# A recurrence kernel whose fp32 state is streamed to TensorE as bf16 upper halves of its own words

## The chip, the cores and the metric

The kernel runs on one NeuronCore of a Trainium2 chip. The metric is the device time of one launch in microseconds. Five engines work side by side and meet only through semaphores: TensorE (PE, with its weight loads shown apart as PEld), VectorE (DVE), ScalarE (ACT), GpSimd (POOL) and SyncE (SP), which here starts the transfers.

## The reference, cut to what matters

```
x = x + moe(x, cond)          # 5 branches (4 experts, 1 shared), each gelu(x @ w1 + b1) @ w2 + b2
# then a gated recurrence over the 1024 time steps of x, batch 2, width 256:
def step(h, xs):              # xzt, xrt, xht are the projections of x, vz, vr, vh those of cond
    z  = sigmoid(xzt + h @ U_z + vz)
    r  = sigmoid(xrt + h @ U_r + vr)
    hh = tanh(xht + r * h @ U + vh)
    h_new = (1.0 - z) * h + z * hh
    return (h_new, h_new)
x = x + all h_new
```

Every step needs the state of the step before, so the 1024 steps are a chain. Within a step there are two products that stand one behind the other: `h @ U_r` must be there before `r * h @ U` can start. The product with `U_z` and the work of the experts are beside that chain.

## The kernel before

Features lie on the 128 partitions (width 256 is KC = 2 chunks `k`), batch and time on the free axis. The state of one step is therefore a 128x4 tile (2 chunks, 2 batch entries). The 1024 steps are cut into 64 bodies of 16 steps (`t` 0 to 15), and 4 bodies make a chunk of 64 steps. The experts' work for the next chunk is cut into fp32 matmuls of 128x128 on 128 columns ("units"), which a table deals out over the steps of the present chunk: each step has window 0, ahead of the candidate's product, and window 1, behind it; window 0 takes one unit and window 1 takes two (one, in every eighth step). Of the 1024 steps about 900 have a unit in window 0. Where there is no unit, bf16 matmuls on a constant tile fill the window (L887).

The recurrent weights are held as two fp16 tiles, `u_high` and `u_mid` (value minus `u_high`). The moving operand is held as two fp16 parts as well, HI and LO. A gate is then 8 "high" matmuls (2 output chunks, 2 input chunks, two weight tiles, all on the HI part) and 4 "low" ones (`u_high` on the LO part), all added up in PSUM (L873). The matmuls stream more columns than they need: the columns beyond the first two are zeros and add nothing (`H_FILL` = 20 for h, `FILL` = 56 for r*h).

One step goes as follows. DVE makes the new state three times with the same scan: into `h_parts` as fp16 (HI, L701), into PSUM as fp32 (`h_fresh`, L703), and into the history `h_hist` (L705). It subtracts HI from the PSUM copy to make LO (L708), and halves the state (L710). PE runs the 8 high matmuls of gate r, then 3 of gate z (`early`), waits for LO, and runs the 4 low ones of r. ACT makes the tanh of r (L481). DVE makes r*h twice, as fp16 (L684) and in PSUM as fp32 (`product`, L685), and subtracts for LO (L687). PE runs z's other matmuls, window 0, and then the candidate's 8 high and 4 low matmuls. ACT makes the candidate's tanh, DVE's next scan takes it. Between the two lie DVE's two operations on gate z (L690, L691).

The projected inputs of a body are put into PSUM ahead of the recurrent products by an identity matmul, once per gate and body ("inject", L859). For that GpSimd splits each body's fp32 inputs into three bf16 parts (L372 to L379). GpSimd also adds the finished body to its input (`h_true`, `out_feat`, L387, L392), PE turns it (`turn_body` in step `t` = 1), ACT copies it and SP stores it. GpSimd's third task is to scale the experts' activations (`scale_tile`, L298, 128x128 fp32, two inputs in SBUF).

The order on every engine is the order in which the code is written; nothing is rescheduled. DVE's operations wait on semaphores (`act_done`, `state`), PE's first matmul of each high and each low group on `part_ready`.

Of the kernel before, what the change touches and what calls it, by code (L numbers as in the profile page):

```python
# [44 lines left out]
FILL = 56  # L45
H_FILL = 20
# [3 lines left out]
def moe_gru_kernel(nc, x, cond, gate_w, gate_b, time_w, time_b, ew1, eb1, ew2, eb2, sw1, sb1, sw2, sb2,  # L50
# [45 lines left out]
    UNITS, GELUS, RESIDUALS, PIECES, FIRST_SPLIT = {}, {}, {}, {}, {}  # L96
    for c in range(CH - 1):
        slots = [(c * TC + s, window) for s in range(TC)
                 for window in ((0, 1) if s % 8 == 7 else (0, 1, 1))]
        for kind, f, i in side_work(c):  # L100
# [13 lines left out]
            if kind == PROJECT:  # L114
                after = at[0] + at[1]
                for m in range(KC):
                    PIECES[after + m] = [(f, i, m, b) for b in range(B)]
                FIRST_SPLIT[after + KC] = f
    FIRST_SPLIT = {max(step for step, g in FIRST_SPLIT.items() if g == f): f for f in range(1, CH)}
# [6 lines left out]
    with ctx:  # L126
# [30 lines left out]
        xrest = sb("xrest", [P, GATES * KC, SC])  # L157
        xsplit = sb("xsplit", [P, 3, GATES * KC, SC], BF16)
        h_hist = sb("h_hist", [P, ROUND, 2 * ST])
        h_true = sb("h_true", [P, KC, SC])  # L160
# [32 lines left out]
        HI, LO = range(2)  # L193
        blend = sb("blend", [P, 2 * ST])
        half_h = sb("half_h", [P, ST])
        body_mark = sb("body_mark", [P, 1])
# [10 lines left out]
        product = gate_ps[R][:, AT + ST:AT + 2 * ST]  # L207
        h_fresh = gate_ps[C][:, AT + 2 * ST:AT + 4 * ST]
        h_now = h_hist[:, :, :].rearrange("p s (e two) -> p s e two", two=2)[:, :, :, 1]
        h_fresh_v = h_fresh.rearrange("p (e two) -> p e two", two=2)[:, :, 1]  # L210
# [21 lines left out]
        pool_passed = sem("pool_passed")  # L232
# [29 lines left out]
        split_ready = sem("split_ready")  # L262
# [7 lines left out]
        body_h = sem("body_h")  # L270
        body_added = sem("body_added")
        h_unscaled = sem("h_unscaled")
# [4 lines left out]
        PARTS_STEP, STATE_STEP = 4, 6  # L277
# [24 lines left out]
        def _(sp):  # L302
# [6 lines left out]
            sp.sem_inc(out_written, 2 * 16)  # L309

# [12 lines left out]
            def store_body(n):  # L323

                sp.wait_ge(turned_copied, n + 2)
# [14 lines left out]
            sp.wait_ge(out_written, (CH * BODIES + 1) * 2 * 16)  # L340
# [3 lines left out]
        def _(pool):  # L344
# [10 lines left out]
            pool.sem_inc(split_ready, 1)  # L355
            pool.memset(out_feat[:, :, :], 0.0).then_inc(body_added, 1)
            CHAIN0, PER_SPLIT = 1, 3

            def wait_apart(semaphore, value):

                pool.wait_ge(semaphore, value)
                pool.sem_inc(pool_passed, 1)

            def split(c, j):

                n = c * BODIES + j
                chain = n * PER_SPLIT + CHAIN0
                src = xpart[:, c % 2, :, j * SC:(j + 1) * SC]
                if j == 0:
                    pool.wait_ge(xp_ready, (c + 1) * (GATES * KC * B) + 1)  # L370
                wait_apart(injected, n + 1)
                pool.tensor_copy(xsplit[:, 0, :, :], src).then_inc(pool_chain, 1)  # L372
                wait_apart(pool_chain, chain + 1)
                pool.tensor_tensor(xrest[:, :, :], src, xsplit[:, 0, :, :],
                                   ALU.subtract).then_inc(pool_chain, 1)
                wait_apart(pool_chain, chain + 2)
                pool.tensor_copy(xsplit[:, 1, :, :], xrest[:, :, :]).then_inc(pool_chain, 1)
                pool.wait_ge(pool_chain, chain + 3)
                pool.tensor_tensor(xsplit[:, 2, :, :], xrest[:, :, :], xsplit[:, 1, :, :],  # L379
                                   ALU.subtract).then_inc(split_ready, 1)  # L380

            def add_body(n):

                first = n % 2 * STEPS
                wait_apart(body_h, n + 1)
                for k in range(KC):
                    pool.tensor_scalar(h_true[:, k, :].rearrange("p (s b) -> p s b", b=B),  # L387
                                       h_now[:, first:first + STEPS, k * B:(k + 1) * B],
                                       h_unscale[:, :], None, ALU.mult).then_inc(h_unscaled, 1)
                wait_apart(h_unscaled, KC * (n + 3))  # L390
                wait_apart(turned, n + 1)
                pool.tensor_tensor(out_feat[:, :, :], h_true[:, :, :],  # L392
                                   feat[:, :, n * SC:(n + 1) * SC], ALU.add
                                   ).then_inc(body_added, 1)

# [18 lines left out]
            pool.wait_ge(scales_made, 1)  # L414
            pool.wait_ge(gate_scales_made, 2)
            split(0, 0)

            for step in range(T):
                n, t = divmod(step, STEPS)
                c, j = divmod(n, BODIES)  # L420
                if t == 0 and n > 0:
                    add_body(n - 1)
                if t == 3 and j < BODIES - 1:
                    split(c, j + 1)
                if step in FIRST_SPLIT:
                    split(FIRST_SPLIT[step], 0)
# [3 lines left out]
            add_body(CH * BODIES - 1)  # L430


        @block.scalar
        def _(act):
# [50 lines left out]
            def input_part(c, g, m, b):  # L485

                if m == 0 and b == 0:
                    act.wait_ge(xp_done, c * GATES + (g + 1))
                    if g == 0:
                        act.wait_ge(split_ready, max(c - 1, 0) * BODIES + 1)  # L490
# [30 lines left out]
            for step in range(T):  # L521
# [4 lines left out]
                if step % STEPS == 5:  # L526
                    copy_rows(step // STEPS)
                for piece in PIECES.get(step, ()):
                    input_part(*piece)
            copy_rows(CH * BODIES)  # L530
# [3 lines left out]
        def _(dve):  # L534
# [10 lines left out]
            dve.memset(p_parts[:, :, :, :], 0.0)  # L545
            dve.memset(h_parts[:, :, :, :], 0.0).then_inc(part_ready, PARTS_STEP)
            dve.memset(h_hist[:, :, :], 0.0)
            dve.sem_inc(h_unscaled, 2 * KC)
# [122 lines left out]

            def gru_body(n):
                first = n * STEPS
                for t in range(STEPS):
                    gate0 = (first + t) * GATES
                    s0 = (first + t + 1) * STATE_STEP
                    sq = lambda ap: ap.rearrange("p (m b) -> p m b", b=B)
                    tr, tz = sq(tanh_r), tanh_z
                    prev = sq(h_now[:, (first + t - 1) % ROUND, :])
                    p = lambda i: p_parts[:, i, :, 0:B]  # L680
# [9 lines left out]
                    dve.tensor_scalar(blend_v[:, :, 0], tz, 1.0, half_s[:, :], ALU.add, ALU.mult).then_inc(state, 1)  # L690
                    dve.scalar_tensor_tensor(blend_v[:, :, 1], tz, 1.0, half_h[:, :], ALU.subtract, ALU.mult  # L691
                                             ).then_inc(state, 1)
# [5 lines left out]
                    dve.wait_ge(state, s0 + 3)  # L698
                    if t == 0:
# [275 lines left out]
```

## Time and profile before

| | us |
|---|---|
| median of three runs | 2120.41 (2115.2 to 2125.93) |
| the profiled execution, as timed | 2111.95 |
| its span, first to last instruction | 2110.1 |
| first scan of the recurrence to the last | 85.94 to 2104.12 |

Busy shares of the span: PE 98%, PEld 86%, DVE 57%, ACT 35%, POOL 19%. Matmuls are pipelined, and a matmul of some 20 columns stands in the trace for about 0.18 us although the next one starts 0.025 us behind it; so PE's 98% doesn't say that PE has no time left. Starts are what is read below. An fp32 matmul stands in the trace as two records, each with its own weight load.

### The profile page before, as it was taken

Reading aid. Unit: us, or ns where it says so; the run is one execution under the profiler, and the core shown is the slowest. Engines: PE = TensorE matmul, PEld = TensorE weight load, DVE = VectorE, ACT = ScalarE, POOL = GpSimd, SP = SyncE. Lnnn points to the kernel's source line nnn. Section 1 sums busy time; section 2 is a strip of 40 time slices with the busy share of each in tenths; the row PEclk is TensorE's granted clock in tenths of the full one; section 3 lists DMA queues with packets and bytes.
Section 4 is the critical chain, followed back from the end, with each engine's and each line's share of the span. In section 5 each row is a group of like instructions: output and inputs, shape, how many; then the busy total and the mean of one; then the engine's idle time right before and its main releaser. Section 6 shows DMA issues by size and latency. Waiting matters only on the chain.

```text
span 2110.1 us, 105994 instructions
## 1 busy us (share of the span) xinstructions
PE 2069.1 (98%) x43624; PEld 1817.8 (86%) x43624; DVE 1201.6 (57%) x10446; ACT 732.4 (35%) x3977; POOL 395.9 (19%) x931
## 2 busy tenths in 40 slices
PE   7999999999999999999999999999999999999998
PEld 6998988989888898988888888898988889888665
DVE  6455555555555555555555555555555555555555
ACT  2433333333333333333333333333333333333222
POOL 3121212121121211212122121211212122120010
PEclk8999999999999999999999999999999999999999
DMA  8000000000000000000000000000000000000000
GB/s 285 2 4 5 5 4 5 4 4 5 5 4 5 5 4 5 5 4 5 5 4 4 5 4 4 4 4 4 5 5 4 5 4 4 5 5 4 4 4 4
DMA packets 16931, 23.90 MB, mean 11 GB/s; under 512 B 3584, under 2 KB 15159, under 8 KB 16444
## 3 DMA queue, kind: packets, MB, share of 16 engines
q1 hardware_dynamic: 15280, 17.05, 2.5%
q8 instruction: 341, 5.59, 1.1%
q14 instruction: 146, 1.20, 0.2%
q10 hardware_dynamic: 1164, 0.07, 0.0%
HBM read 15.01 MB, written 2.10 MB: 8 GB/s over the span
## 4 chain that ended last, share of the span: by engine, by line
PE 94%; issue 2%; DVE 2%; ACT 1%; POOL 0%; POOLq 0%; DVEq 0%; ACTq 0%
PE c_ps L873 21%; PE r_ps L873 19%; PE y_ps L822 17%; PE up_ps L806 17%; PE z_ps L873 14%; PE xp_ps L833 2%; PE up_ps L887 2%; PE xp_ps L887 1%; DVE p_parts L684 1%; ACT r_ps L481 1%; PE rows_ps L854 1%; DVE h_parts L701 1%; DVE hidden L298 0%; ACT c_ps L481 0%; PE y_ps L795 0%
## 5 line engine op out<-in xcount | busy, mean ns | idle before, releaser
L873 PE MATMUL z_ps<-h_parts,u_high 128*128 128x20 f16 x8192 | 566.6, 178 | 0.0
L873 PE MATMUL r_ps<-h_parts,u_high 128*128 128x20 f16 (+1 forms) x8192 | 545.8, 172 | 10.4 <-DVE h_parts L701 0.2
L873 PEld LDWEIGHTS r_ps<-h_parts,u_high 128*128 128x128 f16 x8192 | 419.6, 96 | 154.9 <-DVE h_parts L701 86.3
L873 PE MATMUL c_ps<-p_parts,u_high 128*128 128x56 f16 (+1 forms) x8192 | 532.0, 178 | 11.0
L822 PE MATMUL y_ps<-hidden,down_w 128*128 128x128 f32 x2560 | 524.9, 301 | 4.5 <-DVE hidden L298 4.5
L806 PE MATMUL up_ps<-feat,up_w 128*128 128x128 f32 x2560 | 527.1, 302 | 0.0
L873 PEld LDWEIGHTS c_ps<-p_parts,u_high 128*128 128x128 f16 x8192 | 418.3, 96 | 106.5 <-DVE p_parts L684 33.6
L684 DVE SCALAR_TENSOR_TENSOR p_parts<-r_ps,h_hist 128x4 f16<-128x4 f32 x1024 | 168.4, 164 | 483.8 <-ACT r_ps L481 483.8
L873 PE MATMUL z_ps<-h_parts,u_mid 128*128 128x20 f16 x4096 | 438.3, 178 | 0.0
L873 PEld LDWEIGHTS z_ps<-h_parts,u_high 128*128 128x128 f16 x8192 | 423.5, 95 | 0.0
L481 ACT ACTIVATE r_ps<-r_ps 128x4 f32<-128x4 f32 x1024 | 161.8, 158 | 640.0 <-PE r_ps L873 636.1
L701 DVE TENSOR_TENSOR_SCAN h_parts<-c_ps,blend 128x8 f16<-128x8 f32 x1024 | 178.2, 174 | 344.7 <-ACT c_ps L481 340.4
L822 PEld LDWEIGHTS y_ps<-hidden,down_w 128*128 128x128 f32 x2560 | 367.2, 190 | 5.9 <-issue 3.4
L806 PEld LDWEIGHTS up_ps<-feat,up_w 128*128 128x128 f32 x2560 | 369.5, 191 | 0.4 <-issue 0.2
L481 ACT ACTIVATE c_ps<-c_ps 128x4 f32<-128x4 f32 x1024 | 161.8, 158 | 584.4 <-PE c_ps L873 584.4
L873 PE MATMUL c_ps<-p_parts,u_mid 128*128 128x56 f16 x4096 | 350.2, 187 | 0.0
L873 PE MATMUL r_ps<-h_parts,u_mid 128*128 128x20 f16 x4096 | 336.6, 178 | 0.0
L873 PEld LDWEIGHTS z_ps<-h_parts,u_mid 128*128 128x128 f16 x4096 | 295.6, 96 | 0.0
L873 PEld LDWEIGHTS c_ps<-p_parts,u_mid 128*128 128x128 f16 x4096 | 260.7, 96 | 0.7
L873 PEld LDWEIGHTS r_ps<-h_parts,u_mid 128*128 128x128 f16 x4096 | 256.5, 97 | 0.0
L476 ACT ACTIVATE hidden<-up_ps,small_cols 128x128 f32<-128x128 f32 x640 | 234.5, 366 | 41.0 <-PE up_ps L806 39.9
L690 DVE TENSOR_SCALAR blend<-z_ps,half_s 128x4 f32<-128x4 f32 x1024 | 218.9, 214 | 0.0
(137 smaller groups left out, 2274.8 us busy)
## 6 DMA issues: line engine op xcount, KB each, us to landing
up_w<-in_L_cond_ew SPq DMA_DIRECT2D x4, 1024.0 KB, 12.0
down_w<-in_L_cond_ew SPq DMA_DIRECT2D x4, 1024.0 KB, 13.2
x_rows<-in_x SPq DMA_DIRECT2D x8, 256.0 KB, 5.1
out<-out_rows SPq DMA_DIRECT2D x128, 16.0 KB, 1.8
up_w<-in_L_cond_sw SPq DMA_DIRECT2D x1, 1024.0 KB, 15.7
down_w<-in_L_cond_sw SPq DMA_DIRECT2D x1, 1024.0 KB, 11.8
cf<-in_L_cond_C_r SPq DMA_DIRECT2D x1, 256.0 KB, 5.9
cf<-in_L_cond_C_z SPq DMA_DIRECT2D x1, 256.0 KB, 6.1
```

Of the source, the lines that this page charges most:

```text
L476: act.activation(hidden[:, i % LAG, :], up_ps[i % 2][:, 0:COLS], ACT.Gelu_apprx_tanh, bias=small_cols[:, ROW_B1 + e * HT + j:ROW_B1 + e * ...
L481: act.activation((c_now, tanh_r, tanh_z)[(g + 1) % GATES].rearrange("p (m b) -> p m b", b=B), gate_v[g][:, :, step % STEPS, :], ACT.Tanh, ...
L684: dve.scalar_tensor_tensor(p(HI), tr, 1.0, prev, ALU.add, ALU.mult).then_inc(part_ready, 1)
L690: dve.tensor_scalar(blend_v[:, :, 0], tz, 1.0, half_s[:, :], ALU.add, ALU.mult).then_inc(state, 1)
L701: dve.tensor_tensor_scan(h_parts[:, HI, 0, :], cand, blend[:, :], 0.0, ALU.mult, ALU.add).then_inc(part_ready, 1)
L806: last = mm(up_ps[i % 2][:, 0:COLS], up_w[:, e, k, j * P:(j + 1) * P], feat[:, k, f * COLS:(f + 1) * COLS], start=(k == 0), stop=(k == KC ...
L822: last = mm(y_ps[:, m * COLS:(m + 1) * COLS], down_w[:, e, j, m * P:(m + 1) * P], hidden[:, i % LAG, :], start=False, stop=(m == KC - 1), ...
L833: last = mm(xp_ps[:, m * COLS:(m + 1) * COLS], wx[:, g, k, m * P:(m + 1) * P], feat[:, k, f * COLS:(f + 1) * COLS], start=(m == 0 and k == 0),
L854: last = pe.transpose(rows_ps[0:SC, k * P:(k + 1) * P], out_feat[:, k, :], ident[:, :])
L873: return mm(gate_ps[g][:, m * SC + t * B:m * SC + t * B + width], w[:, g, k, m * P:(m + 1) * P], moving, start=False, stop=i == LO and k = ...
L887: mm(idle_ps[:, 0:IDLE_FILL[window]], ident16[:, :], keep_warm[:, 0:IDLE_FILL[window]], start=True, stop=True, skip_group_check=True)
```

## The change

TensorE now streams the state and r*h out of the fp32 words themselves. DVE writes the state as fp32 into `h_words` (one word in each group of eight, the rest zeros), and PE reads the same bytes as bf16 from the upper half of that word on: 14 bf16 values, the first being the value's upper half and the others zeros, for each of two batch entries. The low part is the fp32 word minus its own bf16 view, as fp16.

```
-        p_parts = sb("p_parts", [P, 2, KC, FILL], F16)
-        h_parts = sb("h_parts", [P, 2, FILL // B, 2 * ST], F16)
+        p_words = sb("p_words", [P, ST + 1, WORDS])
+        h_words = sb("h_words", [P, ST + 1, 2 * WORDS])
+        p_low = sb("p_low", [P, ST + 1, 2 * WORDS], F16)
+        h_low = sb("h_low", [P, ST + 1, 2 * WORDS], F16)
...
+        high = lambda words: words[:, :, :].bitcast(BF16)
+        p_moving, h_moving = high(p_words)[:, :, 1:1 + RUN], high(h_words)[:, :, 2 * WORDS + 1:2 * WORDS + 1 + RUN]
...
-                    dve.scalar_tensor_tensor(p(HI), tr, 1.0, prev, ALU.add, ALU.mult).then_inc(part_ready, 1)
-                    dve.scalar_tensor_tensor(sq(product), tr, 1.0, prev, ALU.add, ALU.mult).then_inc(state, 1)
-                    dve.wait_ge(state, s0 + 1)
-                    dve.tensor_tensor(p(LO), sq(product), p(HI), ALU.subtract).then_inc(part_ready, 1)
+                    dve.scalar_tensor_tensor(p_full, tanh_r, 1.0, h_now[:, (first + t - 1) % ROUND, :],
+                                             ALU.add, ALU.mult).then_inc(part_ready, 1)
+                    dve.wait_ge(part_ready, parts0 + 1)
+                    dve.tensor_tensor(p_rest, p_full, p_high, ALU.subtract).then_inc(part_ready, 1)
...
+                    if n > 0 and 2 <= t < 2 + KC:
+                        output(n - 1, t - 2)
...
-                    dve.tensor_tensor_scan(h_parts[:, HI, 0, :], cand, blend[:, :], 0.0, ALU.mult, ALU.add
+                    dve.tensor_tensor_scan(h_pairs, cand, blend[:, :], 0.0, ALU.mult, ALU.add
                                            ).then_inc(part_ready, 1)
-                    dve.tensor_tensor_scan(h_fresh, cand, blend[:, :], 0.0, ALU.mult, ALU.add
-                                           ).then_inc(state, 1)
                     dve.tensor_tensor_scan(h_hist[:, (first + t) % ROUND, :], cand, blend[:, :], 0.0, ALU.mult, ALU.add
                                            ).then_inc(state, 1)
-                    dve.tensor_tensor(h_parts[:, LO, 0, :], h_fresh, h_parts[:, HI, 0, :],
-                                      ALU.subtract).then_inc(part_ready, 1)
-                    dve.tensor_scalar(half_h[:, :], h_fresh_v, -0.5, None, ALU.mult).then_inc(state, 1)
+                    dve.wait_ge(part_ready, parts0 + 3)
+                    dve.tensor_tensor(h_rest, h_full, h_high, ALU.subtract).then_inc(part_ready, 1)
+                    dve.tensor_scalar(half_h[:, :], h_full, -0.5, None, ALU.mult).then_inc(state, 1)
```

PE's matmuls on h, on r*h and z's low ones now have 28 columns, 2 runs of 14. The two batch entries stay interleaved in PSUM, so one run writes every second fp32 word. The weights stay fp16; the high part beside them is bf16. The injection is one fp32 identity matmul on the projected input itself, and GpSimd's splits are gone. The addition of the finished body is two DVE operations (`output`, at `t` = 2 and 3 of the next body), and `turn_body` stands at `t` = 5.

```
+                last = mm(gate_ps[g][:, 0:KC * SC], ident[:, :],
+                          xpart[:, c % 2, g * KC:(g + 1) * KC, j * SC:(j + 1) * SC],
+                          start=True, stop=True, skip_group_check=True)
...
+                    cols = gate_ps[g][:, at:at + B * run].rearrange("p (f b) -> p b f", b=B)
+                    last = mm(cols, w[:, g, k, m * P:(m + 1) * P], part[:, k * B:(k + 1) * B, 0:run], start=False,
+                              stop=products is LOW_PRODUCTS and k == KC - 1, skip_group_check=True)
...
-                    early = 0 if t == 0 else 3
-                    for product in HIGH_PRODUCTS[:early]:
-                        recur(Z, t, h_parts, HI, product, H_FILL)
                     pe.wait_ge(part_ready, before_n + 4)
-                    for product in LOW_PRODUCTS:
-                        last_mm = recur(R, t, h_parts, LO, product, B)
-                    last_mm.then_inc(preact, 1)
-                    for product in HIGH_PRODUCTS[early:]:
-                        recur(Z, t, h_parts, HI, product, H_FILL)
+                    recur(R, t, h_low, LOW_PRODUCTS, 1).then_inc(preact, 1)
+                    recur(Z, t, h_moving, HIGH_PRODUCTS, RUN)
```

What stands where, at the places that matter (a scan stands in these rows as SCALAR_TENSOR_TENSOR). DVE, one whole step, before:

```order
416 L684 SCALAR_TENSOR_TENSOR p_parts<-r_ps,h_hist 128x2x2 [waits state,act_done]
417 L685 SCALAR_TENSOR_TENSOR r_ps<-r_ps,h_hist 128x4
418 L687 TENSOR_TENSOR p_parts<-r_ps,p_parts 128x2x2 [waits state]
419 L690 TENSOR_SCALAR blend<-z_ps,half_s 128x4 [waits act_done]
420 L691 SCALAR_TENSOR_TENSOR blend<-z_ps,half_h 128x4
421 L701 SCALAR_TENSOR_TENSOR h_parts<-c_ps,blend 128x8 [waits state,act_done]
422 L703 SCALAR_TENSOR_TENSOR c_ps<-c_ps,blend 128x8
423 L705 SCALAR_TENSOR_TENSOR h_hist<-c_ps,blend 128x8
424 L708 TENSOR_TENSOR h_parts<-c_ps,h_parts 128x8 [waits state]
425 L710 TENSOR_SCALAR half_h<-c_ps 128x4
```

and of the changed kernel:

```order
408 L632 SCALAR_TENSOR_TENSOR p_words<-r_ps,h_hist 128x4 [waits state,act_done]
409 L635 TENSOR_TENSOR p_low<-p_words 128x4 [waits part_ready]
410 L638 TENSOR_SCALAR blend<-z_ps,half_s 128x4 [waits act_done]
411 L640 SCALAR_TENSOR_TENSOR blend<-z_ps,half_h 128x4 [waits state]
412 L650 SCALAR_TENSOR_TENSOR h_words<-c_ps,blend 128x8 [waits state,act_done]
413 L652 SCALAR_TENSOR_TENSOR h_hist<-c_ps,blend 128x8
414 L655 TENSOR_TENSOR h_low<-h_words 128x4 [waits part_ready]
415 L656 TENSOR_SCALAR half_h<-h_words 128x4
```

Ten operations became eight: the second copy of r*h and the second copy of the state are gone from between the first write and the subtraction.

PE in an ordinary step, from the high matmuls of gate r to its low ones, before:

```order
3024 L873 MATMUL r_ps<-h_parts,u_high 128x20
3025 L873 MATMUL r_ps<-h_parts,u_mid 128x20
3026 L873 MATMUL z_ps<-h_parts,u_high 128x20
3027 L873 MATMUL z_ps<-h_parts,u_mid 128x20
3028 L873 MATMUL z_ps<-h_parts,u_high 128x20
3029 L873 MATMUL r_ps<-h_parts,u_high 128x2 [waits part_ready]
3030 L873 MATMUL r_ps<-h_parts,u_high 128x2 x3
```

and of the changed kernel:

```order
1821 L822 MATMUL r_ps<-h_words,u_high 128x2x14
1822 L822 MATMUL r_ps<-h_words,u_mid 128x2x14
1823 L822 MATMUL r_ps<-h_low,u_high 128x2 [waits part_ready]
1824 L822 MATMUL r_ps<-h_low,u_high 128x2 x3
1825 L822 MATMUL z_ps<-h_words,u_high 128x2x14
1826 L822 MATMUL z_ps<-h_words,u_mid 128x2x14
```

The three matmuls of gate z that stood ahead of the wait now stand behind r's low ones, in front of window 0.

PE in the first step of a body, around the injection for gate z, before:

```order
2827 L873 MATMUL r_ps<-h_parts,u_high 128x20
2828 L873 MATMUL r_ps<-h_parts,u_mid 128x20
2829 L859 MATMUL z_ps<-xsplit,ident16 128x64 x3
2830 L873 MATMUL r_ps<-h_parts,u_high 128x2 [waits part_ready]
2831 L873 MATMUL r_ps<-h_parts,u_high 128x2 x3
```

and of the changed kernel:

```order
1787 L822 MATMUL r_ps<-h_words,u_high 128x2x14
1788 L822 MATMUL r_ps<-h_words,u_mid 128x2x14
1789 L808 MATMUL z_ps<-xpart,ident 128x64
1790 L822 MATMUL r_ps<-h_low,u_high 128x2 [waits part_ready]
1791 L822 MATMUL r_ps<-h_low,u_high 128x2 x3
```

Three bf16 matmuls ahead of r's low ones became one fp32 matmul in the same place.

## Rows read from the trace of the kernel before

**Rows 1.** Timeline, DVE: first and last scan (start us, us, what).

```profile
85.94 0.17 DVE L701 TENSOR_TENSOR_SCAN h_parts<-c_ps,blend 128x8 f16<-128x8 f32 x1 [0.37 <-ACT c_ps L481]
...
2104.12 0.17 DVE L701 TENSOR_TENSOR_SCAN h_parts<-c_ps,blend 128x8 f16<-128x8 f32 x1 [0.34 <-ACT c_ps L481]
```

**Rows 2.** Timeline, DVE, one step, from its scan to the next.

```profile
1013.32 0.17 DVE L701 TENSOR_TENSOR_SCAN h_parts<-c_ps,blend 128x8 f16<-128x8 f32 x1 [0.34 <-ACT c_ps L481]
1013.41 0.17 DVE L703 TENSOR_TENSOR_SCAN c_ps<-c_ps,blend 128x8 f32<-128x8 f32 x1
1013.49 0.15 DVE L705 TENSOR_TENSOR_SCAN h_hist<-c_ps,blend 128x8 f32<-128x8 f32 x1
1013.61 0.17 DVE L708 TENSOR_TENSOR h_parts<-c_ps,h_parts 128x8 f16<-128x8 f32 x1
1013.70 0.15 DVE L710 TENSOR_SCALAR half_h<-c_ps 128x4 f32<-128x4 f32 x1
1014.32 0.17 DVE L684 SCALAR_TENSOR_TENSOR p_parts<-r_ps,h_hist 128x4 f16<-128x4 f32 x1 [0.47 <-ACT r_ps L481]
1014.39 0.16 DVE L685 SCALAR_TENSOR_TENSOR r_ps<-r_ps,h_hist 128x4 f32<-128x4 f32 x1
1014.59 0.16 DVE L687 TENSOR_TENSOR p_parts<-r_ps,p_parts 128x4 f16<-128x4 f32 x1
...
1015.29 0.17 DVE L701 TENSOR_TENSOR_SCAN h_parts<-c_ps,blend 128x8 f16<-128x8 f32 x1 [0.34 <-ACT c_ps L481]
```

**Rows 3.** Timeline, PE, the same step: matmuls of r, z, window 0, candidate.

```profile
1013.55 0.18 PE L873 MATMUL r_ps<-h_parts,u_high 128*128 128x20 f16 x1
...
1013.74 0.18 PE L873 MATMUL r_ps<-h_parts,u_mid 128*128 128x20 f16 x1
...
1013.84 0.24 PE L873 MATMUL r_ps<-h_parts,u_high 128*128 128x2 f16 x4
...
1014.17 0.47 PE L806 MATMUL up_ps<-feat,up_w 128*128 128x128 f32 x2
1014.54 0.20 PE L873 MATMUL c_ps<-p_parts,u_high 128*128 128x56 f16 x1
...
1014.73 0.19 PE L873 MATMUL c_ps<-p_parts,u_mid 128*128 128x56 f16 x1
1014.81 0.25 PE L873 MATMUL c_ps<-p_parts,u_high 128*128 128x2 f16 x4
```

**Rows 4.** Timeline, PE, the first step of a body.

```profile
999.90 0.18 PE L873 MATMUL r_ps<-h_parts,u_mid 128*128 128x20 f16 x1
999.93 0.25 PE L859 MATMUL z_ps<-xsplit,ident 128*128 128x64 bf16 x3
1000.01 0.24 PE L873 MATMUL r_ps<-h_parts,u_high 128*128 128x2 f16 x4
...
1000.50 0.47 PE L806 MATMUL up_ps<-feat,up_w 128*128 128x128 f32 x2
1000.81 0.19 PE L873 MATMUL c_ps<-p_parts,u_high 128*128 128x56 f16 x1
```

**Rows 5.** Fill matmuls: one pair in the timeline; their group by line and shape.

```profile
2103.76 0.59 PE L887 MATMUL up_ps<-keep_warm,ident 128*128 128x512 bf16 x2
...
L887 PE MATMUL up_ps<-keep_warm,ident 128*128 128x512 bf16 x170 | 50.3, 377 | 0.0
```

**Rows 6.** Timeline: DVE and GpSimd operations that overlap, ahead of the recurrence.

```profile
81.12 0.29 DVE L298 TENSOR_TENSOR hidden<-hidden,gate_scale 128x128 f32<-128x128 f32 x1 [0.52 <-ACT hidden L476]
82.02 0.46 DVE L298 TENSOR_TENSOR hidden<-hidden,gate_scale 128x128 f32<-128x128 f32 x1 [0.60 <-ACT hidden L476]
...
81.78 0.55 POOL L379 TENSOR_TENSOR xsplit<-xrest,xsplit 128x192 bf16<-128x192 f32 x1
```

**Rows 7.** GpSimd scaling: one of the step in rows 2, and a group.

```profile
1013.65 0.40 POOL L298 TENSOR_TENSOR hidden<-hidden,expert_w 128x128 f32<-128x128 f32 x1 [1.57 <-ACT hidden L476]
...
L298 POOL TENSOR_TENSOR hidden<-hidden,gate_scale 128x128 f32<-128x128 f32 x235 | 108.3, 461 | 477.5 <-ACT hidden L476 477.5
```

More of the change, by code:

```diff
@@ L354, in _ @@
                                       bass.bass_isa.ReduceOp.max).then_inc(umax_shared, 1)
[L355 to L394, printed above, removed]
             pool.wait_ge(expert_w_made, 1)
@@ L488, in input_part @@
                     act.wait_ge(xp_done, c * GATES + (g + 1))
[L489 to L490 removed]
+                    if g == 0 and c >= 2:
+                        act.wait_ge(injected, (c - 1) * BODIES)
                 act.activation(
@@ L525, in _ @@
                     gelu(f, i)
-                if step % STEPS == 5:
-                    copy_rows(step // STEPS)
+                if step % STEPS == 8 and step > STEPS:
+                    copy_rows(step // STEPS - 1)
                 for piece in PIECES.get(step, ()):
                     input_part(*piece)
-            copy_rows(CH * BODIES)
+            copy_rows(CH * BODIES - 1)
         @block.vector
@@ L724, in _ @@
                 gru_body(n)
+            dve.wait_ge(state, (T + 1) * STATE_STEP)
+            for k in range(KC):
+                output(CH * BODIES - 1, k)
         @block.tensor
@@ L855, in turn_body, with inject @@
                 last.then_inc(turned, 1)
-            def inject(g, last_of_body):
-                for i in range(3):
-                    last = mm(gate_ps[g][:, 0:KC * SC], ident16[:, :],
-                              xsplit[:, i, g * KC:(g + 1) * KC, :].rearrange("p k n -> p (k n)"),
-                              start=(i == 0), stop=(i == 2), skip_group_check=True)
-                if last_of_body:
+            def inject(g, n):
+                c, j = divmod(n, BODIES)
+                if g == R and j == 0:
+                    pe.wait_ge(xp_ready, (c + 1) * (GATES * KC * B) + 1)
+                last = mm(gate_ps[g][:, 0:KC * SC], ident[:, :],
+                          xpart[:, c % 2, g * KC:(g + 1) * KC, j * SC:(j + 1) * SC],
+                          start=True, stop=True, skip_group_check=True)
+                if g == C:
                     last.then_inc(injected, 1)
@@ L866, in _, with recur @@
             LOW_PRODUCTS = [(m, k, u_high) for m in range(KC) for k in range(KC)]
-            def recur(g, t, part, i, product, width):
-                m, k, w = product
-                moving = (p_parts[:, i, k, 0:width] if part is p_parts else
-                          h_parts[:, i, 0:width // B, (2 * k) * B + 1:(2 * k + 2) * B:2])
-                return mm(gate_ps[g][:, m * SC + t * B:m * SC + t * B + width],
-                          w[:, g, k, m * P:(m + 1) * P], moving, start=False,
-                          stop=i == LO and k == KC - 1, skip_group_check=True)
+            def recur(g, t, part, products, run):
+                for m, k, w in products:
+                    at = m * SC + t * B
+                    cols = gate_ps[g][:, at:at + B * run].rearrange("p (f b) -> p b f", b=B)
+                    last = mm(cols, w[:, g, k, m * P:(m + 1) * P], part[:, k * B:(k + 1) * B, 0:run], start=False,
+                              stop=products is LOW_PRODUCTS and k == KC - 1, skip_group_check=True)
+                return last
             def gap_work(n, t, window):
-                if t == 1 and window == 1:
-                    turn_body(n)
+                if t == 5 and window == 1 and n > 0:
+                    turn_body(n - 1)
                 units = UNITS.get((n * STEPS + t, window), ())
```

102 lines of the change are left out of this document (36 added, 66 removed).

## The prediction, made before the changed kernel ran

> **What bounds the kernel now.** I read the timeline first, since 98% for PE is made of overlapping records. The first scan of the recurrence starts at 85.94 and the last at 2104.12 [rows 1]: 1023 steps of 1.973 us, which is 96% of the span, so the question is one step. DVE's rows of one step [rows 2] beside PE's [rows 3], as distances from the scan's start: scan 0; PE's first r matmul 0.23, the eighth 0.42; the subtraction L708 0.29; r's low matmuls 0.52; r*h (L684) 1.00; its second copy (L685) 1.07; its subtraction (L687) 1.27; the candidate's high matmuls 1.22 to 1.41, its low ones 1.49; next scan 1.97. Each link starts a fixed distance behind the one before. From the subtraction L708 to r's low matmuls it is 0.23, from these to L684 0.48 (four matmuls, ACT's tanh, DVE), from L687 to the candidate's low matmuls 0.22, from these to the next scan 0.48. The step is a chain of latencies through DVE, PE and ACT. PE is close behind it, though: its eight r matmuls end at 0.42, and I note that three z matmuls fill the time to 0.52.
>
> **DVE's second copies, the gain.** Before, L708 starts 0.29 behind the scan, because it waits for the second scan (0.09 later, 0.17 long, then 0.03) [rows 2]. Afterwards it needs the first scan alone: 0.17 + 0.03 = 0.20 to 0.21. Its bounds are 0.19 (if a scan into SBUF takes the 0.15 of L705) and 0.23 (if the spread-out fp32 writes cost 0.02). Likewise L687 started 0.27 behind L684 and will start 0.16 + 0.035 = 0.20 behind it. That is 0.08 and 0.07 off the chain. L708's and L687's own durations I keep at 0.17 and 0.16.
>
> **PE takes over at three places.** R's low matmuls are ready at 0.205 + 0.23 = 0.435; PE has issued the eight high ones at 0.42 + 0.025 = 0.445. So 0.445, against 0.52 before: 0.075 gained. With nothing waited for, the four follow at 0.025 each, 0.005 less than behind a wait. So r*h starts at 0.445 + 0.475 = 0.92. The candidate's high matmuls are ready 0.22 later, at 1.14. PE by then has to issue 4 low r, 12 z (three of them moved behind the wait by the change) and window 0. Those are 16 x 0.025 = 0.40, so the fp32 unit starts at 0.845. In rows 4 a unit keeps PE from 1000.50 to 1000.81, 0.31, and the next matmul really waits for it there. So they start at 1.155, PE 0.015 late. This holds in the 900 steps with a unit in window 0. The eight took 0.19 with a longer first gap behind a wait [rows 3]; with none, 7 x 0.026 = 0.18. Hence the low ones at 1.155 + 0.18 + 0.025 = 1.36 (they are ready at 0.92 + 0.20 + 0.22 = 1.34), and the next scan at 1.36 + 0.47 = 1.83. A step is 1.83 instead of 1.97: 0.14 x 1023 = **143 us gained**. Window 1 keeps its 0.6 us between the candidate's low matmuls and the next scan plus 0.23, so its two units stay hidden.
>
> **The injection, a loss.** In a body's first step the three bf16 matmuls move r's low ones to 0.11 behind the last high one, against 0.025 [rows 4]; this was hidden but for about 0.03, since LO was late anyway. An fp32 matmul is two passes with two weight loads; a unit's 0.31 less 0.05 for 64 instead of 128 columns in its last pass is 0.26. It stands on the path: r's low matmuls come at 0.42 + 0.27 = 0.69 instead of 0.445, 0.245 later. The injection for the candidate stands ahead of window 0's unit and puts two more fp32 weight loads (0.31 less a last pass of about 0.10, so 0.21) and a gap of 0.02 in front of the candidate: 0.23. Together 0.47 x 64 = 30 us, less 0.03 x 64 = 2 before: **28 us lost**. The injection for r is in the last step's window 1, which has only one unit (0.31 + 0.26 in 0.6): nothing.
>
> **Edits at nothing.** GpSimd's splits and body additions were never waited for in the loop. DVE's `output` (two operations on 32 columns, below 0.29, the 128-column row of rows 6) fits in the 0.5 us between L691 and the scan. `turn_body` costs at `t` = 5 what it cost at `t` = 1. The tail loses one GpSimd stage of some 0.6 us. The added wait ahead of L640 is on DVE's own earlier operation and is met. The head is unchanged.
>
> **The unknown term: 28 columns in every second PSUM word.** No matmul of before writes PSUM with a step. Twenty columns (r) and fifty-six (candidate) both go by 0.025 to 0.027 [rows 3]; long ones cost (0.59 - 0.377) / 512 = 0.42 ns a column [rows 5]. If a stepped column is worth one, 28 stay at 0.025. If it is worth two, they are the 56 of before, 0.026. On the bounding path lie 8 r, 12 z and 8 candidate matmuls, so 1 ns each is 0.028 x 1024 = 29 us. I take the mean of the two readings, 0.3 ns, 9 us. Lower end 0, upper end open (below). The mixed types (fp16 weights, bf16 moving) are not in the trace either. The nearest rows are bf16 matmuls among fp16 ones at no visible cost [rows 4]; I take 0.
>
> **Sum.** 2112 - 143 + 28 - 1 + 9 = 2005 us in terms of the profiled execution. The median shown is 1.004 of that execution (2120.4 / 2112), so **2013 us**. Within this case: scans shorter by 0.02 give -20, matmuls slower by 0.5 ns more +15, strided DVE operations 0.03 longer at one place +30: 1978 to 2060.
>
> **Rival 1, slower: the stepped PSUM writes.** One mechanism: a stepped column is worth three or more. Then 28 of them are at least 84 columns, 28 x 0.42 = 12 ns above the 56-column matmul; 12 x 29 = 345, so about 2360. It decides from 4 ns: 108 us are to be eaten up at 29 us per ns, so at matmuls above 0.029 to 0.030 the kernel is slower. For it: no row excludes it. Against it: half the rate is the plainest price of writing one word of each two. I give 0.16 to this, and 0.08 to something between (2120 to 2200). The Trainium skill (Advanced Engine Details and Errata, PSUM Cachelines) says that PSUM lines hold two fp32 values and that any non-contiguous pattern slows matmuls significantly. No run here shows it yet; by its line size a line per value is the factor two, which by the numbers above is 2022, and "significantly" read as more is this rival.
>
> **Rival 2: DVE and GpSimd in each other's way.** A DVE operation on two SBUF tensors takes 0.29 alone and 0.46 beside a GpSimd operation that runs to 82.33, 0.15 before DVE's end [rows 6]. Before, all small DVE operations of a step had one tensor in PSUM; now L635 and L655 have both in SBUF, and L656 goes from SBUF to SBUF. GpSimd scales in some 450 steps (235 of one kind, about as many of the other), 0.40 to 0.46 each [rows 7], from 0.33 behind the scan. L655 would run from 0.21 to 0.37, so it is first; L635 at 1.12 comes after GpSimd's end at 0.79 or a little more. L656 (from 0.29) may lose the race and end at 0.95, which delays L684 by 0.03 to 0.1: 15 to 45 us, 2028 to 2058. Were L655 itself caught, it would be 0.37 x 450 = 165 us, 2180. Chance 0.10 for a visible cost, nearly all of it the smaller one. The Trainium skill (SBUF — State Buffer, Who interferes with whom) states this rule, a lock held for the whole instruction whenever DVE has two SBUF inputs and GpSimd reads SBUF; rows 6 agree with it.
>
> **Rival 3: the change doesn't do what it says.** The separate copies were started 0.08 apart, overlapped; if each new operation on spread-out words (scan, r*h, both subtractions) is 0.03 longer, 0.06 to 0.12 of the 0.14 is gone: 2070 to 2125. The three kinds of scan differ by only 0.02 [rows 2], which speaks against it. Chance 0.08.
>
> **How the numbers follow.** Forecast 0.58; rival 1 0.16, its milder form 0.08; rival 2 0.10; rival 3 0.08. The range from 1975 to 2190 takes all but the strong form of rival 1 and the tails, about 0.8. This kernel's runs can tell 0.5%, 10 us, from no change. Faster by more: 0.58 + 0.10 + 0.07 = 0.75 less 0.02 for the tails, 0.73; within: 0.04; slower: 0.16 + 0.07 = 0.23.
>
> **What would show it.** In the profile of the changed kernel: L655 0.20 to 0.21 behind the scan (a GpSimd row beside a longer L655 or L656 is rival 2); r's low matmuls directly behind its eighth; starts of 28-column matmuls 0.025 to 0.026 apart (0.030 or more is rival 1); L635 0.20 behind L632; the first step of a body about 0.47 longer than the others; 1.83 from scan to scan. What would make it wrong most easily is the spacing of the matmuls, since PE now bounds three places of the step.

## The result and the profile after

| | before | changed |
|---|---|---|
| median, us | 2122.23 (4 runs, 2115.2 to 2125.93) | 2024.10 (4 runs, 2022.93 to 2025.53) |
| profiled execution, span | 2110.1 | 2022.6 |
| first to last scan | 85.94 to 2104.12 | 84.71 to 2017.92 |
| mean from scan to scan | 1.973 | 1.890 |

The changed kernel takes 0.954 of the time, 95% interval 0.952 to 0.957: 4.6% faster. The forecast was 2013, the range 1975 to 2190. Of the 87.5 us of span, 85 come from the recurrence; the tail gives 1.3, and the head's 1.2 is less than it differs by among the kernels below that share it (first scan at 83.3 to 86.3).

The medians are 98 us apart, the two profiled executions 88 (2111.95 and 2024.38). Of 11 later runs of the kernel before, the time and the mean granted clock are on record: from 2110.1 us at 0.996 to 2129.7 at 0.979, longer with each lower clock but for one run at 0.999 (2111.4). The changed kernel's stood at 0.996 to 1.000. So some 10 us of the medians' distance go with the clock, and the change itself is worth about 4.1%; why the kernel before loses clock is open.

DVE of one step in the timeline of the changed kernel (start us, us, engine, line, operation, out<-in), to be held against [rows 2]:

```profile
1009.11 0.18 DVE L650 TENSOR_TENSOR_SCAN h_words<-c_ps,blend 128x8 f32<-128x8 f32 x1 [0.30 <-ACT c_ps L422]
1009.20 0.16 DVE L652 TENSOR_TENSOR_SCAN h_hist<-c_ps,blend 128x8 f32<-128x8 f32 x1
1009.32 0.18 DVE L655 TENSOR_TENSOR h_low<-h_words 128x4 f16<-128x4 f32 x1
...
1010.04 0.17 DVE L632 SCALAR_TENSOR_TENSOR p_words<-r_ps,h_hist 128x4 f32<-128x4 f32 x1 [0.47 <-ACT r_ps L422]
1010.24 0.18 DVE L635 TENSOR_TENSOR p_low<-p_words 128x4 f16<-128x4 f32 x1
...
1010.97 0.18 DVE L650 TENSOR_TENSOR_SCAN h_words<-c_ps,blend 128x8 f32<-128x8 f32 x1 [0.30 <-ACT c_ps L422]
```

The state's subtraction starts 0.21 behind the scan (0.29 before), that of r*h 0.20 behind the product (0.27 before), and the step takes 1.86 (1.97 before). PE of the same step, against [rows 3]:

```profile
1009.35 0.20 PE L822 MATMUL r_ps<-h_words,u_high 128*128 128x28 bf16 x1
...
1009.54 0.19 PE L822 MATMUL r_ps<-h_words,u_mid 128*128 128x28 bf16 x1
1009.56 0.25 PE L822 MATMUL r_ps<-h_low,u_high 128*128 128x2 f16 x4
1009.68 0.19 PE L822 MATMUL z_ps<-h_words,u_high 128*128 128x28 bf16 x1
...
1009.99 0.47 PE L767 MATMUL y_ps<-hidden,down_w 128*128 128x128 f32 x2
1010.29 0.19 PE L822 MATMUL c_ps<-p_words,u_high 128*128 128x28 bf16 x1
...
1010.50 0.24 PE L822 MATMUL c_ps<-p_low,u_high 128*128 128x2 f16 x4
```

R's low matmuls stand 0.02 behind its last high one, where they stood 0.10 behind it before: PE has no gap there any more. The candidate's high ones stand 0.30 behind the fp32 unit, the distance at which a waiting matmul follows a unit in [rows 4]; they are held by PE, not by DVE. The first step of a body, against [rows 4]:

```profile
1020.77 0.19 PE L822 MATMUL r_ps<-h_words,u_mid 128*128 128x28 bf16 x1
1020.80 0.41 PE L808 MATMUL z_ps<-xpart,ident 128*128 128x64 f32 x2
1021.05 0.25 PE L822 MATMUL r_ps<-h_low,u_high 128*128 128x2 f16 x4
...
1021.47 0.41 PE L808 MATMUL c_ps<-xpart,ident 128*128 128x64 f32 x2
1021.72 0.44 PE L751 MATMUL up_ps<-feat,up_w 128*128 128x128 f32 x2
1021.99 0.19 PE L822 MATMUL c_ps<-p_words,u_high 128*128 128x28 bf16 x1
```

The low matmuls of r come 0.28 behind the last high one (0.11 before). The scans around it are at 1020.34 and 1022.67, 2.33 apart.

### The profile page after: what moved, and what is told of

The parts are those of the page before. It is cut to its first block, busy times and chain, and to the rows that moved or that the text cites. A ratio compares the mean times of both kernels' runs of the same rounds, so it can differ in the third digit from the quotient of the medians.

```text
span 2022.6 us, 102778 instructions
## 1 busy us (share of the span) xinstructions
PE 1988.2 (98%) x43359; PEld 1816.3 (90%) x43430; DVE 1142.4 (56%) x8464; ACT 737.2 (36%) x3976; POOL 217.8 (11%) x482
## 4 chain that ended last, share of the span: by engine, by line
PE 96%; DVE 2%; issue 1%; ACT 1%; DMA 0%; SPq 0%; POOL 0%; DVEq 0%; ACTq 0%
PE r_ps L822 20%; PE y_ps L767 17%; PE up_ps L751 17%; PE z_ps L822 17%; PE c_ps L822 16%; PE xp_ps L778 2%; PE up_ps L836 2%; PE xp_ps L836 1%; PE c_ps L808 1%; PE z_ps L808 1%; PE rows_ps L800 1%; DVE h_words L650 1%; ACT c_ps L422 1%; PE r_ps L808 1%; DVE hidden L294 1%
## 5 line engine op out<-in xcount | busy, mean ns | idle before, releaser
L822 PE MATMUL r_ps<-h_words,u_high 128*128 128x28 bf16 x4096 | 362.8, 190 | 9.3 <-DVE h_words L650 0.3
L822 PE MATMUL c_ps<-p_words,u_high 128*128 128x28 bf16 x4096 | 354.0, 188 | 1.2
L822 PE MATMUL r_ps<-h_words,u_mid 128*128 128x28 bf16 x4096 | 350.2, 187 | 0.0
L822 PE MATMUL z_ps<-h_words,u_mid 128*128 128x28 bf16 x4096 | 350.2, 187 | 0.0
L822 PE MATMUL c_ps<-p_words,u_mid 128*128 128x28 bf16 x4096 | 350.2, 187 | 0.0
L822 PE MATMUL z_ps<-h_words,u_high 128*128 128x28 bf16 x4096 | 349.4, 187 | 0.0
L822 PEld LDWEIGHTS c_ps<-p_words,u_high 128*128 128x128 f16 x4096 | 264.0, 96 | 25.3 <-DVE p_words L632 24.1
L822 PE MATMUL z_ps<-h_low,u_high 128*128 128x28 f16 x4096 | 270.8, 187 | 0.0
L822 PEld LDWEIGHTS r_ps<-h_words,u_mid 128*128 128x128 f16 x4096 | 260.0, 96 | 0.0
L822 PEld LDWEIGHTS c_ps<-p_words,u_mid 128*128 128x128 f16 x4096 | 259.3, 96 | 0.7
```

The source lines that it names most:

```text
L822: last = mm(cols, w[:, g, k, m * P:(m + 1) * P], part[:, k * B:(k + 1) * B, 0:run], start=False, stop=products is LOW_PRODUCTS and k == KC ...
```

## The experiments

All are changes to the changed kernel; its time is called "2024". An interval is given where there are several times; of the others there is one, and the changed kernel's own four lie within 0.13%.

**The stepped PSUM writes.** Three kernels vary the columns or the step.

```
-RUN = 2 * WORDS - 2
+RUN = 10
```

> Each run of columns is 10 instead of 14, so a recurrent matmul streams 20 columns into every second PSUM word instead of 28. Theory (a stepped column costs as much as two): 20 count as 40, below what the 56 of before cost, so starts go from 0.026 to 0.025 us apart; the 28 matmuls between the scan and the candidate's low ones save 0.02 to 0.03 a step, 2024 becomes 1998 to 2008. Rival (the spacing of 0.026 comes from the mixed types or from the words' distance, not from the columns): no change, 2024.

Measured: 2012.85 us, 0.948 of the kernel before (interval 0.941 to 0.955). And with 44 columns:

```
-WORDS = 8
+WORDS = 12
```

> Each run of columns is 22 instead of 14 (words 12 apart instead of 8), so 44 stepped columns. Theory (a stepped column costs as much as two): 44 count as 88, about 0.42 ns each, starts 0.037 to 0.040 us apart, +0.3 to +0.4 us a step, 2330 to 2430 us. Rival (a stepped column costs one): 44 are still below 56, starts stay at 0.026, 2024 us.

Measured: 2368.2 us. The z group of the two kernels, and of the changed one between them, by line and shape (busy us, mean ns of one):

```profile
L822 PE MATMUL z_ps<-h_words,u_high 128*128 128x20 bf16 x4096 | 337.2, 179 | 0.0
```

```profile
L822 PE MATMUL z_ps<-h_words,u_high 128*128 128x28 bf16 x4096 | 349.4, 187 | 0.0
```

```profile
L822 PE MATMUL z_ps<-h_words,u_high 128*128 128x44 bf16 x4096 | 444.5, 210 | 0.0
```

A matmul of 28 stepped columns stands in the trace for 187 ns, which is what the 56 unstepped columns of the kernel before took (0.19 in [rows 3]), and 20 stepped ones for 179, as 20 unstepped ones did (0.18). The starts say the same. Within the z group they are in the mean 25.0 ns apart with 20 columns, 25.8 with 28 and 38 with 44. These rows are of the 44:

```profile
1009.54 0.21 PE L822 MATMUL z_ps<-h_words,u_high 128*128 128x44 bf16 x1
1009.58 0.21 PE L822 MATMUL z_ps<-h_words,u_mid 128*128 128x44 bf16 x1
1009.62 0.21 PE L822 MATMUL z_ps<-h_words,u_high 128*128 128x44 bf16 x1
```

At 0.42 ns a column [rows 5], 88 columns are 37 ns: a column into every second PSUM word costs about as much as two. That rests on one size above the floor of 25 ns; 44 columns without a step were not run, but the 56 of the kernel before stand 25.8 ns apart. The short run gained 11 us where 16 to 26 were expected. Its step went from 1.857 to 1.846 only. R's low matmuls were by then waiting for DVE's subtraction (its start 0.21, its length 0.177, and 0.06 until they start: 0.45), and the last of the four starts at 0.536 in both kernels, so the spacing of r's eight no longer counted. In the same way the candidate's four start 0.015 earlier, but the last of them only 0.008.

The third kernel takes the step out of PSUM and puts the jump on the reading side:

```
-                    cols = gate_ps[g][:, at:at + B * run].rearrange("p (f b) -> p b f", b=B)
-                    last = mm(cols, w[:, g, k, m * P:(m + 1) * P], part[:, k * B:(k + 1) * B, 0:run], start=False,
+                    cols = gate_ps[g][:, at:at + B * run].rearrange("p (f b) -> p f b", b=B)
+                    last = mm(cols, w[:, g, k, m * P:(m + 1) * P], part[:, k * B:(k + 1) * B, 0:run].rearrange("p b f -> p f b"), start=False,
```

> The two batch entries are interleaved on the moving side instead of in PSUM: PSUM is written without a step, and the moving operand is read with a jump of 32 or 64 bytes from column to column. Theory (the PSUM step is what makes 28 columns cost like 56, and jumps on the reading side are free): starts 0.025 apart, 1998 to 2008 us. Rival (jumps on the reading side cost more than the step in PSUM): starts over 0.030 apart, above 2060 us.

Measured: 2111.9 us. The theory fell: its z matmuls start 28.2 ns apart, more than the 25.8 with the step in PSUM, and the ordinary step is 1.915. The rival's 30 was not reached, though its time was. In ten stretches of 7 to 17 us the granted clock fell to its lower level of 1.2 GHz, which it does nowhere in the changed kernel's recurrence. The 972 steps outside them are longer than the changed kernel's by 53 us in all, 0.055 each; the 51 steps in them by 35, of which 32 go with the clock. Stretches of this kernel's profile (the column behind POOL is the granted clock):

```profile
182.00:300.00 118.00, 117.31 (x2559) 109.88 (x2557) 66.83 (x496) 42.76 (x236) 13.35 (x31) 1.00 0.02 4
301.00:318.00 17.00, 17.00 (x262) 16.31 (x262) 7.26 (x54) 4.83 (x27) 0.80 (x2) 0.51 0.01 2
318.00:430.00 112.00, 111.31 (x2421) 104.00 (x2422) 62.92 (x468) 40.13 (x220) 12.93 (x30) 1.00 0.02 4
```

In the 17 us at a mean of 0.51 PE got 15.4 matmuls a microsecond done, in the stretch before 21.7. Before the fall at 301 us PE was busy for 117.3 of 118 us, as in the changed kernel (497.0 of 500). All ten falls begin at the same place of a chunk of 64 steps, from 0.3 us ahead of to 1.1 us behind the scan that ends its third body, some 6 us behind two steps whose windows hold bf16 fill matmuls in place of fp32 units. The changed kernel has the same work there and keeps its clock; why it fell here and not there is open.

**DVE's second copies.** Both are put back, and the subtractions wait for them:

```
+                    dve.scalar_tensor_tensor(product, tanh_r, 1.0, h_now[:, (first + t - 1) % ROUND, :],
+                                             ALU.add, ALU.mult).then_inc(copied, 1)
+                    dve.wait_ge(copied, 2 * (first + t) + 1)
-                    dve.wait_ge(part_ready, parts0 + 1)
...
+                    dve.tensor_tensor_scan(h_fresh, cand, blend[:, :], 0.0, ALU.mult, ALU.add
+                                           ).then_inc(copied, 1)
...
-                    dve.wait_ge(part_ready, parts0 + 3)
+                    dve.wait_ge(copied, 2 * (first + t) + 2)
```

> The second copy of r*h and the second scan into PSUM are put back between the first write and the subtraction, which waits for them; nothing reads them otherwise. Theory (the gain is these two operations off the chain): subtraction of the state 0.29 behind the scan instead of 0.21, that of r*h 0.27 behind instead of 0.20, r's low matmuls at 0.53 instead of 0.45; a step of 1.99 instead of 1.857, about 2155 us. Rival (PE bounds the step by itself and would have given the gain without this): the second copies hide behind PE, at most 1.90 a step, below 2070 us.

Measured: 2160.1 us, 1.017 of the kernel before (interval 1.010 to 1.025). The ordinary step is 2.00. The rival is out: PE alone gives nothing, and the two copies are worth 136 us, more than the whole difference between the kernels. With the copies back the step is 0.033 longer than the 1.967 before, so the rest of the change costs that much. The rows place it: r's last low matmul starts at 0.616 instead of 0.602, and the candidate's low ones 0.236 instead of 0.220 behind the start of their subtraction, which takes 0.178 instead of 0.164. DVE in one step of this kernel, with GpSimd's operation beside it:

```profile
1012.04 0.18 DVE L655 TENSOR_TENSOR_SCAN h_words<-c_ps,blend 128x8 f32<-128x8 f32 x1 [0.35 <-ACT c_ps L425]
...
1012.32 0.18 DVE L662 TENSOR_TENSOR h_low<-h_words 128x4 f16<-128x4 f32 x1
1012.41 0.43 DVE L663 TENSOR_SCALAR half_h<-h_words 128x4 f32<-128x4 f32 x1
1013.04 0.17 DVE L635 SCALAR_TENSOR_TENSOR p_words<-r_ps,h_hist 128x4 f32<-128x4 f32 x1 [0.20 <-ACT r_ps L425]
...
1012.36 0.46 POOL L297 TENSOR_TENSOR hidden<-hidden,gate_scale 128x128 f32<-128x128 f32 x1 [1.88 <-ACT hidden L420]
```

The subtraction is 0.28 behind the scan, as wanted. The halving of the state, due at 0.37 and now behind GpSimd's start at 0.32, takes 0.43 instead of 0.16 and ends 0.02 behind GpSimd; 454 of the 1024 are like this. It costs nothing: their steps are 2.00 long, as the others. This answers the milder half of rival 2 of the prediction, in which the held halving was to delay the next product: here it ends at 0.80, and the product starts at 1.00.

**The fp32 injection.** First with one bf16 matmul per gate on inputs kept as bf16:

```
-        xpart = sb("xpart", [P, 2, GATES * KC, COLS])
+        xpart = sb("xpart", [P, 2, GATES * KC, COLS], BF16)
...
-                last = mm(gate_ps[g][:, 0:KC * SC], ident[:, :],
+                last = mm(gate_ps[g][:, 0:KC * SC], ident16[:, :],
```

> The projected inputs are kept as bf16 and injected by one bf16 matmul per gate and body, so the low 16 bits of the projected inputs are left out. Theory (the fp32 injection costs 0.47 us in each body's first step): the step from a body's last scan to the next body's first, 2.33 us in the changed kernel against 1.86 in the others, falls to 1.86 to 1.90; 27 to 30 us less, 1994 to 1997 us. Rival (the first step is long for another reason, such as the wait for the state or for the projected inputs): it stays above 2.2 us and the time above 2018.

Measured: 1997.2 us, and a body's last scan is 1.906 from the next body's first (2.327 in the changed kernel). The 27 us are the injection's. Then the fp32 matmul of gate z moved ahead:

```
-                    if t == 0:
-                        inject(Z, n)
...
                         inject(R, n + 1)
+                        pe.wait_ge(state, (n + 1) * STEPS * STATE_STEP + 2)
+                        inject(Z, n + 1)
...
+            inject(Z, 0)
```

> The fp32 injection for gate z is moved from between r's high and low matmuls to the end of the last step's window 1, behind the one for r. Theory (PE has no time left in these two steps, so its work only moves): 0.24 us less behind the scan, but window 1 then holds 0.33 + 0.27 + 0.24 in 0.63 and gives 0.2 back; 2018 to 2026 us. Rival (what costs is the place on the path alone): 64 x 0.24 = 15 us less, 2009 us.

Measured: 2016.65 us, just below the theory's 2018. The step is mostly 2.162 instead of 2.327. Of the 0.24 to 0.25 that the path alone would have gained, 0.165 are left, since r's first matmul, behind the fuller window 1, starts at 0.332 instead of 0.232. In 14 of the 63 such steps it is 2.28 or more; the mean is 2.184 instead of 2.314, which makes 8 us.

**GpSimd beside DVE.** Less of it, and more of it:

```
...
+            if engine is not dve_engine[0]:
+                part = hidden[:, i % LAG, 0:B]
+                engine.tensor_tensor(part, part, expert_w[:, e, :], ALU.mult).then_inc(scaled, 1)
+                return
...
```

> GpSimd scales only the first two columns of each tile instead of 128, so nearly all of its scaling is left out. Theory (GpSimd's work meets DVE's two SBUF-to-SBUF operations in a handful of steps only): 2020 to 2024 us. Rival (each GpSimd operation costs DVE some time): 450 steps x 0.03 or more, below 2010 us.

Measured: 2020.7 us: GpSimd's scaling costs the changed kernel 0 to 4 us in all. In the changed kernel three of DVE's rows of L635, L655 and L656 are held. One is this (DVE and GpSimd timeline):

```profile
120.61 0.18 DVE L650 TENSOR_TENSOR_SCAN h_words<-c_ps,blend 128x8 f32<-128x8 f32 x1 [0.29 <-ACT c_ps L422]
...
120.82 0.39 DVE L655 TENSOR_TENSOR h_low<-h_words 128x4 f16<-128x4 f32 x1
...
120.78 0.40 POOL L294 TENSOR_TENSOR hidden<-hidden,expert_w 128x128 f32<-128x128 f32 x1 [1.46 <-ACT hidden L417]
```

GpSimd started 0.17 behind the scan here, 0.04 ahead of the subtraction, which then lasted until GpSimd was done. In 459 of 467 cases GpSimd starts 0.32 behind the scan, when the subtraction runs already.

```
                         scale_tile(pool, f, i)
...
+                        pool.tensor_tensor(scrap[:, :], ones[:, :], ident[:, :], ALU.mult).then_inc(scrapped, 1)
```

> Behind each scaling GpSimd runs a second operation of the same size on three other SBUF tiles, so it is busy from 0.32 to about 1.15 to 1.25 us behind the scan instead of 0.32 to 0.78. Theory (a DVE operation with two SBUF inputs waits while GpSimd runs): the subtraction of r*h, due at 1.13, is held until GpSimd ends in the 450 steps with a scaling, rows of 0.2 to 0.3 us instead of 0.178; 5 to 40 us more, 2029 to 2064 us. Rival (they don't get in each other's way): 2024 us.

Measured: 2022.9 us, no difference. The second operation starts at 0.68 to 0.75 and ends at 1.13 or 1.14 in 227 steps and at 1.19 or 1.20 in 231. The subtraction of r*h, at 1.13, was held in 5 steps of 1024. So in some 230 steps GpSimd ran on for 0.06 into the subtraction, which took its 0.178 all the same. DVE and GpSimd of one such step:

```profile
1010.59 0.18 DVE L642 TENSOR_TENSOR p_low<-p_words 128x4 f16<-128x4 f32 x1
...
1010.14 0.46 POOL L378 TENSOR_TENSOR scrap<-ones,ident 128x128 f32<-128x128 f32 x1
```

The expectation had the end about right; what it had wrong is that so short an overlap would cost something. With two added operations, on a buffer of two halves:

```
                         scale_tile(pool, f, i)
+                        for _ in range(2):
+                            if scraps[0] > 1:
+                                pool.wait_ge(scrapped, scraps[0] - 1)
+                            pool.tensor_tensor(scrap[:, scraps[0] % 2, :], ones[:, :], ident[:, :], ALU.mult).then_inc(scrapped, 1)
+                            scraps[0] += 1
```

> As with the doubled GpSimd work, but with two added operations behind each scaling, so GpSimd runs from 0.32 to about 1.5 us behind the scan and the last of its three operations starts at about 1.03 to 1.1, ahead of the subtraction of r*h at 1.13. Theory (whoever starts first holds the other up to its end): that subtraction takes 0.4 to 0.6 us instead of 0.178 in about 450 steps, +0.25 to +0.4 us each, 2130 to 2200 us. Rival (the few long rows seen so far had another reason): below 2035 us.

Measured: 2085.7 us. The subtraction of r*h was held in 262 steps, not in 450: in the others the third operation started behind it. DVE of one such step in the timeline, with GpSimd's row of the two added operations:

```profile
1001.12 0.17 DVE L658 TENSOR_TENSOR_SCAN h_words<-c_ps,blend 128x8 f32<-128x8 f32 x1 [0.30 <-ACT c_ps L430]
...
1002.29 0.40 DVE L643 TENSOR_TENSOR p_low<-p_words 128x4 f16<-128x4 f32 x1
...
1001.79 0.87 POOL L378 TENSOR_TENSOR scrap<-ones,ident 128x128 f32<-128x128 f32 x2
```

And the group of all these subtractions, by line (busy us, mean ns of one, idle us before them):

```profile
L643 DVE TENSOR_TENSOR p_low<-p_words 128x4 f16<-128x4 f32 x1024 | 248.7, 243 | 34.8
```

262 x 0.26 is 68 us; 61 were measured. The held ones end 0.03 behind GpSimd's operation. So a GpSimd operation that starts first holds the subtraction up to its own end, except where its end is as near as the 0.06 above. The changed kernel is not hurt because of where GpSimd's operation happens to start.

**A version that beats both.** It has 20 columns (as in the first experiment), gate z's injection at the body's end (as above), and lighter windows around the body's border:

```
-RUN = 2 * WORDS - 2
+RUN = 10
...
-                 for window in ((0, 1) if s % 8 == 7 else (0, 1, 1))]
+                 for window in {0: (1, 1), 15: (0,)}.get(s % STEPS, (0, 1, 1))]
...
-                if not units:
+                if not units and (t, window) not in ((0, 0), (STEPS - 1, 1)):
```

> A version meant to beat both: 20 instead of 28 columns; the fp32 injection for gate z in the last step's window 1; no unit in that window and none in window 0 of a body's first step (they move to the windows that had one unit in every eighth step). Theory: 11 us for the columns as measured alone, 7 for the injection as measured alone, and the body's first step down from 2.16 (with the earlier injection) to about 1.86, 0.3 x 64 = 19 us; 1984 to 1990 us. Rival (the moved units cost elsewhere what they save there): 2000 us or more.

Measured: 1984.9 us, 0.940 of the kernel before (0.938 to 0.941). And the same without the change of `RUN`, so with the 28 columns kept:

> As the version meant to beat both, with the 28 columns kept. Theory: 11 us above it, 1994 to 2001 us, the step from a body's last scan to the next body's first at 1.86 to 1.92 us. Rival (the moved units cost what they save): 2010 us or more.

Measured: 1995.5 us. In both the step at the border is 1.85 long, like the others. The moved units cost next to nothing where they went (the other steps' mean is 1.853, against 1.851 in the first experiment), and the fp32 injection is free as long as it fills windows that are empty.

## Why the prediction was right, point by point

- **What bounds the kernel**: right. Each link of the chain came in the same order, only earlier; putting the two copies back gave 2160.
- **DVE's second copies**: 0.205 and 0.20 were forecast, 0.21 and 0.20 came. The durations of the subtractions were a little off: with both operands in SBUF and spread out they take 0.178 and 0.177 instead of 0.163 and 0.167.
- **PE takes over**: right in kind at all three places. R's low matmuls start at 0.452 (0.445 forecast). The four then take 0.084 instead of 0.075, because by the longer subtraction the second of them still comes to a short wait (0.031 behind the first). The candidate's high matmuls start at 1.175 (1.155), its low ones at 1.384 (1.36), the next scan at 1.857 (1.83).
- **The unknown term**: the step of the sum that was mis-sized. I took 0.3 ns per stepped matmul; it is 0.8 ns (25.8 against 25.0), the upper of my two readings, "two columns each". The readings as I wrote them, 0.025 and 0.026, have the mean 0.5 ns, not 0.3, so 6 us of this were a wrong sum. 0.5 ns x 29 is 15 us of the 19 that the forecast for the profiled execution (2005, measured 2024.4) is short; the 0.009 of the four low matmuls is 9 more. Together these are a little more than the gap; the unit ahead of the candidate kept PE 0.304, not 0.31, which gives 6 back.
- **The median**: that 2013 is only 11 us off is in part luck. I multiplied by 1.004, the ratio of median to profiled execution of the kernel before; the changed kernel's median (2024.1) is its profiled execution (2024.4), so these 8 us had no ground.
- **The injection**: 0.47 in a body's first step was forecast and 0.470 came (2.327 - 1.857). With one bf16 matmul in its place, 27 us were gained. What I hadn't seen is that it could be had for nothing by emptying two windows.
- **Edits at nothing**: right. The step with `turn_body` is 0.05 longer at `t` = 5 as it was at `t` = 1; `output` takes 0.24 in the gap ahead of the scan.
- **Rival 1** (a stepped column is worth three or more) is out by the spacings, 25.8 ns at 28 columns and 38 at 44. What saved the change is that 28 doubled columns are no more than the time that a matmul of 20 takes anyway, within 0.8 ns. The margin was small: at 44 columns the same kernel is 11% slower than before. The Trainium skill (Advanced Engine Details and Errata, PSUM Cachelines) says that any non-contiguous pattern slows matmuls significantly. The 44 columns agree; at 28 it is 0.8 ns, and at 20 nothing. The factor two is my inference from its line size of two fp32 values, and the 38 ns fit it.
- **Rival 2**: the lock is real (rows of 0.39 and 0.43), and its price here is 0 to 4 us. I had its mild form at 15 to 45 us. In the changed kernel the halving starts at 0.29, ahead of GpSimd's 0.32, and was held once. Where it is held, in the copies' experiment, it ends 0.02 behind GpSimd and not a whole 0.16, as I had it, so DVE still idles 0.20 ahead of the product.
- **Rival 3**: of its four operations the two subtractions are 0.010 and 0.014 longer, the scan and r*h 0.001, not 0.03; the halving is 0.01 longer too.

## What to carry to other kernels

On a chain of short dependent operations count starts and waits, not busy time: an operation between a write and its reader costs its place in the queue and its length, here 0.08 us for a scan of 8 elements, 1024 times. When such a gap closes, look at once at what stood in it: the z matmuls that filled it now stand in front of the candidate's, and PE is late there. The candidate's low matmuls start 0.254 behind their subtraction, against 0.236 with the copies put back; without that, an estimate from these two, the change would have gained 0.018 more a step. What else a change brings is in the difference as well: the copies are worth 0.143 a step, the change gained 0.110, and the 0.033 between them is mostly that r's low matmuls and the second subtraction take longer. Two engines that can lock each other out should be placed by when they start, and that place should be looked at again whenever the chain between them is shortened.

## What the runs showed of the hardware that was not expected

- A matmul whose PSUM output goes to every second fp32 word takes about twice the time per column, once that is more than the 25 ns of a small one: 44 columns start 38 ns apart in the mean, where 88 x 0.42 is 37, and 28 columns 25.8. Reading the moving operand with a jump of 32 or 64 bytes at every column costs more than that at 28 columns (28.2 against 25.8 ns).
- The kernel that reads with jumps lost the upper clock again and again, and of the profiled executions it alone did so in the recurrence: four slices of its profile's 40, the first aside, stand below full. This row of its page is the granted clock in tenths:

```profile
PEclk8999989999999899999999999899999989999999
```

- fp16 weights with a bf16 moving operand, in alternation with fp16 moving operands, cost nothing that can be seen: 25.0 ns apart at 20 columns, as with fp16 alone.
- A DVE operation of 0.178 us with two SBUF inputs was not lengthened by a GpSimd operation that ended 0.06 behind its start; in the tripled experiment all that started ahead of it and ended 0.22 or more behind its start held it, and it ended 0.03 behind them (rows of 0.26 to 0.46).
